# Dense layers of a graph network: biases by one-row products on TensorE, VectorE and ScalarE straight from PSUM

## The reference

```
combined = concat(views)                       # N x 512, views = relu(bn(agg)) * softmax
z  = combined @ W1 + b1                        # N x 256
z  = (z - mean(z)) / sqrt(var(z) + eps)        # per node
z  = relu(z * ln_scale + ln_bias)
x1 = layernorm(x + z @ W2 + b2)                # N x 128
h1 = relu(x1 @ W.T + b)                        # N x 128, read by the second message passing
```

## Time and profile before

| | |
|---|---|
| median of the runs | 5179.13 us |
| the profiled execution | 5165.81 us, span 5164.1 us |
| dense stage, first `sum_z` to the last Relu of h1 | 2680.3 to 3044.8 us of the span |
| TensorE busy over the span | 66% |
| VectorE, ScalarE, GpSimd busy | 60%, 30%, 66% |
| mean granted TensorE clock | 0.814 of full speed |

### The profile page before, as it was taken

The page is one execution under the profiler, slowest core; times in us unless marked ns, Lnnn a source line. Parts: engine busy times, 40 slices in busy tenths (PEclk is TensorE's granted clock), DMA queues, the critical chain, the costliest instruction groups (busy, mean ns, idle before and its releaser), DMA issues. The chain is left out here.

```text
span 5164.1 us, 87939 instructions
## 1 busy us (share of the span) xinstructions
PE 3404.1 (66%) x21754; PEld 2934.1 (57%) x21755; DVE 3119.2 (60%) x9027; ACT 1526.2 (30%) x4303; POOL 3392.2 (66%) x3492
## 2 busy tenths in 40 slices
PE   5677777777777539999918865555555555555555
PEld 3455555555555438888817755555555555555555
DVE  3888888888888798888766653333333333333332
ACT  3455555555555435555504420000000000000000
POOL 2777777777777636666500037777777777777776
PEclk8788888888888769999959987777777777777777
DMA  4343434434434337777773422222222222222221
GB/s 129 113 110 108 110 109 109 111 108 108 111 108 109 93 90 204 204 206 203 194 228 124 130 86 58 59 59 59 59 59 60 59 58 60 59 59 59 59 60 52
DMA packets 419507, 535.02 MB, mean 104 GB/s; under 512 B 186917, under 2 KB 312433, under 8 KB 419447
## 3 DMA queue, kind: packets, MB, share of 16 engines
q0 software_dynamic: 111408, 227.67, 18.4%
q1 hardware_dynamic: 270918, 272.21, 17.3%
q10 hardware_dynamic: 37121, 34.46, 2.1%
HBM read 365.54 MB, written 168.49 MB: 103 GB/s over the span
## 5 line engine op out<-in xcount | busy, mean ns | idle before, releaser
L2172 POOL DMA_INDIRECT g_h_row<-h_table,g_at_dst x1666 | 1588.4, 953 | 511.0 <-issue 503.4
L2218 PE MATMUL g_ps<-g_h_row,g_same 128*128 128x129 f32 x6664 | 1212.0, 361 | 896.6 <-DMA g_h_row<-h_table,g_at_dst 896.6
L2218 PEld LDWEIGHTS g_ps<-g_h_row,g_same 128*128 128x128 f32 x6664 | 1150.2, 271 | 958.6 <-DMA g_h_row<-h_table,g_at_dst 683.5
L788 POOL DMA_INDIRECT w_src_row<-node_table,w_at_src x1099 | 1112.8, 1013 | 339.4 <-issue 279.8
L1464 POOL DMA_INDIRECT w_row_in<-node_table,w_at_late x471 | 473.3, 1005 | 291.5 <-issue 163.9
L1450 PE MATMUL w_pw<-w_weighed,w_row_in 128*128 128x224 f32 x3140 | 631.5, 356 | 48.7 <-DMA w_row_in<-gathered 38.0
L2241 DVE TENSOR_SCALAR g_code_i<-g_record 128x17 int32<-128x17 f32 x98 | 18.4, 188 | 1061.7 <-DMA g_h_row<-h_table,g_at_dst 1059.7
L1450 PEld LDWEIGHTS w_pw<-w_weighed,w_row_in 128*128 128x128 f32 x3140 | 586.7, 190 | 97.3 <-issue 92.3
L2186 ACT ACTIVATE g_ydev<-g_ydev 128x2 f32<-128x2 f32 (+2 forms) x50 | 10.0, 203 | 2100.4 <-DVE g_ydev L2290 2100.4
L2255 DVE TENSOR_SCALAR g_same<-g_iota_f,g_lo,g_record 128x256 f32<-128x256 f32 x1666 | 552.8, 408 | 103.8 <-PE g_ps L2218 103.7
L899 PE MATMUL w_pr<-ident_b,w_slots 128*56 128x128 bf16 x1570 | 167.9, 247 | 493.0 <-ACT w_apart L841 456.7
(11 more groups left out here) (267 smaller groups left out, 4364.8 us busy)
## 6 DMA issues: line engine op xcount, KB each, us to landing
gathered<-w_src_row SPq DMA_DIRECT2D x157, 462.0 KB
w_row_in<-gathered SPq DMA_DIRECT2D x157, 462.0 KB
aggT<-w_total SPq DMA_DIRECT2D x157, 224.0 KB
g_h_row<-h_table,g_at_dst POOLq DMA_INDIRECT x1666, 2.5
aggT<-w_zeros ACTq DMA_DIRECT2D x157, 159.5 KB
a_in<-aggT SPq DMA_DIRECT2D x50, 500.0 KB, 5.6
a_again<-aggT SPq DMA_DIRECT2D x24, 1024.0 KB, 6.8
w_src_row<-node_table,w_at_src POOLq DMA_INDIRECT x1099
```

The source lines that it names most:

```text
L788: pool.indirect_dma_start(src_row[q.h][:, k, :], None, node_table, bass.IndirectOffsetOnAxis(ap=at_src[q.h][:, k:k + 1], axis=0),).then_in ...
L2172: pool.indirect_dma_start(h_row[s][:, j, 0:F], None, h1_table, bass.IndirectOffsetOnAxis(ap=at_dst[s][:, j:j + 1], axis=0),).then_inc(rows ...
L2218: last = nc.tensor.matmul(ps[q.h][t][:, :], same[s][:, j, t * P:(t + 1) * P], h_row[s][:, j, :], start=(s == 0 and j == 0), stop=(s == 1 a ...
```

## The change

`sum_z` and `sum_h1` each get one more product per tile: the row `ones` against the row of the bias, accumulated onto the sum in PSUM, so that PSUM then holds z and h1 with their biases. The add on VectorE in `norm_z` is left out: moments and normalisation read `pz`. The function `add_h1` is left out: `relu_h1` reads `px` and writes `h1`, and takes over the wait for the store two quads back. Since `pz` is now read until the normalisation, `sum_z` waits for `z_ready` in place of `z_dev`, and `turn_x1` for `h1_ready` in place of `h1_added`.

```diff
@@ sum_z
-                        after(pe, z_dev, q.c - 1)
+                        after(pe, z_ready, q.c - 1)
                         for t, n in enumerate(sizes(q)):
                             for v in range(VIEWS):
-                                last = nc.tensor.matmul(pz[q.h][0:n, t, :],
-                                                        view[q.h][:, v, t * P:t * P + n], w1[:, v, :],
-                                                        start=(v == 0), stop=(v == VIEWS - 1))
+                                nc.tensor.matmul(pz[q.h][0:n, t, :],
+                                                 view[q.h][:, v, t * P:t * P + n], w1[:, v, :],
+                                                 start=(v == 0), stop=False)
+                            last = nc.tensor.matmul(pz[q.h][0:n, t, :], ones[:, 0:n], b1_all[0:1, :],
+                                                    start=False, stop=True)
                         last.then_inc(z_summed, 1)
@@ turn_x1
-                        after(pe, h1_added, q.c)
+                        after(pe, h1_ready, q.c)
@@ sum_h1
-                            last = nc.tensor.matmul(px[0:n, t * P:(t + 1) * P],
-                                                    x1T[:, t * P:t * P + n], l1_wT[:, :],
-                                                    start=True, stop=True)
+                            nc.tensor.matmul(px[0:n, t * P:(t + 1) * P], x1T[:, t * P:t * P + n],
+                                             l1_wT[:, :], start=True, stop=False)
+                            last = nc.tensor.matmul(px[0:n, t * P:(t + 1) * P], ones[:, 0:n],
+                                                    l1_b_all[0:1, :], start=False, stop=True)
@@ relu_h1
-                        act.wait_ge(h1_added, q.c + 1)
+                        act.wait_ge(h1_summed, q.c + 1)
+                        if not (isinstance(q.c, int) and q.c < 2):
+                            act.wait_ge(h1_stored[q.h], landed(q.back(2)))
                         for t, k, n in stretches(q):
-                            last = nc.scalar.activation(h1[q.h][0:n, t:t + k, :],
-                                                        h1[q.h][0:n, t:t + k, :], ACT.Relu)
+                            last = nc.scalar.activation(
+                                h1[q.h][0:n, t:t + k, :],
+                                px[0:n, t * P:(t + k) * P].rearrange("p (t f) -> p t f", t=k), ACT.Relu)
@@ norm_z
-                        for t, k, n in stretches(q):
-                            last = nc.vector.tensor_tensor(
-                                z_n[q.h][0:n, t:t + k, :], pz[q.h][0:n, t:t + k, :],
-                                b1_all[0:n, :].unsqueeze(1).to_broadcast([n, k, Z]), ALU.add)
-                        chain.link(last)
-                        moments(chain, q, z_n[q.h], zstat, zmom, zdev, z_dev)
-                        normed(chain, q, z_n[q.h], z_n[q.h], zmom, zdev, z_root, z_ready)
+                        moments(chain, q, pz[q.h], zstat, zmom, zdev, z_dev)
+                        normed(chain, q, z_n[q.h], pz[q.h], zmom, zdev, z_root, z_ready)
@@ add_h1 and its call: left out
```

More of the change, by code:

```diff
@@ L1791, in resnorm_gnn @@
                          "y_summed", "y_dev", "y_root", "x1_ready", "x1_turned", "x1T_ready",
-                         "h1_summed", "h1_added", "h1_ready", "x_biased")
+                         "h1_summed", "h1_ready", "x_biased")
                 (view_ready, z_summed, z_dev, z_root, z_ready, z_turned, z_relu, y_summed, y_dev,
-                 y_root, x1_ready, x1_turned, x1T_ready, h1_summed, h1_added, h1_ready, x_biased) = (
+                 y_root, x1_ready, x1_turned, x1T_ready, h1_summed, h1_ready, x_biased) = (
                     sem(ctx, n) for n in names)
@@ L2013, in norm_z @@
                             return
-                        chain = Chain(dve, z_step, STEPS * q.c)
+                        chain = Chain(dve, z_step, (STEPS - 1) * q.c)
                         dve.wait_ge(z_summed, q.c + 1)
                         after(dve, z_turned, q.c - 1)
-                        for t, k, n in stretches(q):
-                            last = nc.vector.tensor_tensor(
-                                z_n[q.h][0:n, t:t + k, :], pz[q.h][0:n, t:t + k, :],
-                                b1_all[0:n, :].unsqueeze(1).to_broadcast([n, k, Z]), ALU.add)
-                        chain.link(last)
-                        moments(chain, q, z_n[q.h], zstat, zmom, zdev, z_dev)
-                        normed(chain, q, z_n[q.h], z_n[q.h], zmom, zdev, z_root, z_ready)
-                        assert chain.n == STEPS
+                        moments(chain, q, pz[q.h], zstat, zmom, zdev, z_dev)
+                        normed(chain, q, z_n[q.h], pz[q.h], zmom, zdev, z_root, z_ready)
+                        assert chain.n == STEPS - 1
                     def norm_y(q):
@@ L2041, in norm_y @@
                         assert chain.n == STEPS
[L2043 to L2054, removed]
                     def body(q):
                         norm_z(q)
-                        add_h1(q.back(2))
                         norm_y(q.back(1))
```

## The result

The changed kernel takes 5255.3 us (median of four runs, 5253.3 to 5256.8) against 5180.1 for the kernel before: ratio 1.0147, 95% interval 1.013 to 1.0165, 75 us slower. The forecast was 5206, the range ended at 5238. The direction was right and the size was not. The time is that of the first rival, 5250.

What follows compares the result with a forecast made beforehand. The order of waits in the dense stage was taken to set the pace, no engine being full. 42.0 for `sum_z`'s records, -18.1 for the bias add, +3.0 at the stage's end: +26.9 us, 5206 us; range 5186 to 5238.

Steps and rivals of the forecast that it cites:

- the first rival: In `sum_z` and `sum_h1`, each change of depth empties the array, 0.16 us each; +71 us, 5250; 17 in 100.
- The loop: Dense stage's chain per quad: `sum_z`, bias add, moments, root, view, next `sum_z`; 13.90 us, forecast to become 14.94.
- the bias add: VectorE's add of b1 to z, 1.25 us on the chain; removal gains 0.71 per normal quad, 18.1 us in sum.
- Moments from PSUM: VectorE's moments of z, read from PSUM instead of SBUF: no change in time taken.
- The normalisation from PSUM: VectorE's normalisation of z: even at twice its 1.38 us, it ends near 14.4 and idle VectorE takes it.
- Relu from PSUM and the moved waits: h1's Relu on ScalarE reading PSUM, and waits of `turn_x1`, `sum_z` and the store: cost 0.
- the price of the one-row products in `sum_z`: Eight added records per quad at 0.219 us, 1.75 us with no cover; 42.0 us over 24 intervals.
- that of `sum_h1`: Eight added records of 128 columns per quad in `sum_h1` cost 1.0 us, hidden in TensorE's wait.
- the cover of 0.78 us: TensorE's wait for the view left per quad; once gone, each further microsecond would count in full, 24 us.
- The stage's end: Last quads of the dense stage, drained without overlap: longer `sum_h1` and `sum_y`, together +3.0 us.
- The clock: Granted clock in the dense stage: 0 to -3.4 us and 0 to +3.5 us; taken as 0 for both.
- both dips: Two `sum_z` of 8.86 us in place of 7.17 at granted clock 0.73; may go, 0 to -3.4 us.

Runs made afterwards that it cites:

- e1: Changed kernel with both biases by products over 128 rows of 1/128 in place of one row; 5205.6 us, ratio 1.0018 to the kernel before.
- e6: Kernel before, with z's bias by one bf16 product per tile over 128 rows, split in three parts; h1's add stays on VectorE; 5184.8 us, ratio 0.9989.
- e2: Kernel before, with only z's bias by one-row products and moments from PSUM; h1's bias still added on VectorE; 5246.3 us, ratio 1.0103.
- e4: Kernel before, with only z's bias by one-row products, placed first in their sums, two tiles of different banks together; 5259.8 us, ratio 1.0122.
- e5: Changed kernel with z's bias by products over 64 rows and h1's over 32 rows; one run, 5271 us against 5189 for the kernel before.
- e3: Kernel before, with only h1's bias by one-row products and Relu from PSUM; z's bias still added on VectorE; 5200.2 us, ratio 1.0012.
- e7: Kernel before, with only z's bias by one-row products, placed last in their sums, two tiles of different banks together; 5225.4 us, ratio 1.0072.

## Why the prediction was wrong

- **Read rightly.** The loop, the place of the bias add in it, and that `relu_z` would take its place: the root's waits went from 24 to one. Its gain was taken too small, 0.71 us a quad where e1 and e6 gave 0.93; in the changed kernel that is hidden, since TensorE is the bound. Moments from PSUM cost the same (419 ns against the 414 of the earlier trace rows). The normalisation from PSUM rose from 1.38 to 1.90 us, under the doubling allowed for, and lay in idle time. (Counted from the root at 11.72, the doubled one would end near 14.9 and not 14.4.) Behind Relu from PSUM and the moved waits no new wait shows while the quads run.
- **The step that failed is the price of the one-row products in `sum_z`.** I took "the line's own pace, since in `sum_z` weight loads run under the stream": 1.75 us a quad. They cost 3.08 in the changed kernel and 3.18 in e2. The columns cost what I said (0.215 a record in e4, 0.216 over 128 rows in e1); the weight loads are what doesn't run under the stream at a change of depth, and the next line comes later. Eight changes at 0.17 to 0.19 make the difference. `sum_z` beyond 9.5 us was the sign set down for the first rival; it took 10.09.
- **So did that of `sum_h1`**: 2.3 us in place of 1.0. With that the cover of 0.78 us was gone, TensorE became the bound, and the period is 16.63. The first rival had 16.7 by the same sum, from 0.16 per change; I gave it 17 in 100. That its 5250 lies only 5 us off is in part luck: 0.16 was the whole overlap, where 0.09 of it goes and 0.10 of load comes on top, and it had neither the five quads with the clock dropped nor all of the stage's end.
- **Why I held it unlikely**: from the earlier trace rows I read that the next line starts 0.07 us before the former's end, and took the loss as at most 0.09. The changed kernel shows the same 0.07 at its changes. The reading of that half was right, and the other half, 0.10 for the exposed load, doesn't show in a start against an end. The right comparison would have been the length of the line behind the change: eight records in 1.99 or in 1.89. The rule on the mode change, which I had cited from the Trainium skill's "TensorEngine Tiling (Array Packing)", Key Properties, deserved more than the row that I set against it.
- **The stage's end** took 8.6 us more (3019.43 to 3044.80 before, 3101.93 to 3135.90 after) and not 3.0: the same changes, partly at the lower clock.
- **The clock**: in e1, which has the wait that I forecast (0.73 to 0.89 us), both dips are gone, at the lower end of what I had allowed (0 to -3.4). The changed kernel has no such wait, and its dips came to another line, as the last section shows.
- **The range**: by its own terms it would have ended at 5225 and not at 5222 (11.8 and 7 above 5206); 5255 lies beyond that and beyond 5238.

## What to carry to other kernels

An f32 product of 1, 32 or 64 rows between products of 128 costs, beside its columns, two changes of depth at nearly 0.2 us each; group such products, or fill the rows up, as 128 rows of 1/128 do for a bias. Before work is moved to an engine that has idle time, count whether its wait is cover for one move or for two: z's and h1's products cost 52 and 6 us alone and 75 together. And an instruction on the loop is worth only the time until the next path, here 0.93 of 1.25 us.

## What the runs showed of the hardware

The granted clock fell where TensorE had not been idle. In the changed kernel it dropped in `sum_y`:

```profile
2872.00:2875.00 3.00, 3.00 (x21) 2.20 (x19) 1.97 (x9) 1.69 (x3) 0.00 (x0) 1.00 0.05 18
2875.00:2877.20 2.20, 2.20 (x11) 1.55 (x10) 1.70 (x5) 2.20 (x5) 0.00 (x0) 0.91 0.00 0
2877.20:2880.50 3.30, 3.30 (x17) 3.25 (x17) 0.38 (x1) 1.53 (x3) 0.00 (x0) 0.54 0.00 0
```

TensorE counts as busy all through, yet the clock falls to 0.54, nearly all of the stretch at 1.2 GHz, behind `sum_h1` with its eight changes of depth; `sum_y` then took 3.44 us in place of 2.05. Five quads of 18.3 us in place of 16.6 come from this. e5 has five as well, and in e3, with h1's part alone, `sum_y` takes 3.3 to 3.5 us in three quads. e2, with its eight changes in `sum_z`, shows none. In e4 the clock fell behind one-row products that follow a wait of 0.9 us, in e7 with the same products last it didn't, and in e1, without changes of depth and with nearly the same wait, no quad shows it. In the kernel before it fell in two quads, behind waits of 1.8 to 1.9 us that the other quads had too. What decides it was not tested by itself, and stays open.
